# A Strassen-like fp32 MLP kernel without its 36 opening matmuls on ones

## The reference

```
h = jax.nn.gelu(jnp.einsum('bni,ih->bnh', x, W1) + b1, approximate=False)   # 512 -> 2048
shared_x = jnp.einsum('bnh,ho->bno', h, W2) + b2                             # 2048 -> 384
We_sel = We[indices]                                                         # one of 8 experts per batch
expert_x = jnp.einsum('bnh,bhp->bnp', h, We_sel) + be_sel[:, None, :]        # 2048 -> 128
out = x + jnp.concatenate([shared_x, expert_x], axis=-1)
```

## Time and profile before

| | |
|---|---|
| median of 3 runs | 1239.53 us (1239.34 to 1239.58) |
| the profiled execution, its own time | 1239.52 us |
| span of its profile | 1237.8 us |
| TensorE busy | 1232.1 us (100% of the span) |
| VectorE busy | 940.0 us (76%) |
| ScalarE busy | 742.4 us (60%) |
| TensorE's instructions | 9368 matmuls and 9368 weight loads |

### The profile page before, as it was taken

How to read it: one execution, slowest core, us unless ns; L and a number is a source line. 1 busy time by engine, 2 the same in 40 slices (tenths; PEclk the granted TensorE clock), 3 DMA queues, 4 the chain that set the end, 5 groups by cost and what they waited for, 6 DMA issues and landing times.

```text
span 1237.8 us, 23794 instructions
## 1 busy us (share of the span) xinstructions
PE 1232.1 (100%) x9368; PEld 917.4 (74%) x9368; DVE 940.0 (76%) x1201; ACT 742.4 (60%) x944; POOL 0.2 (0%) x4
## 2 busy tenths in 40 slices
PE   9999999999999999999999999999999999999998
PEld 4456667787787777777777877778778777777775
DVE  7986677877777877768878688787787777777765
ACT  4656556666566665666566566565666656666553
POOL 0000000000000000000000000000000000000000
PEclk9999999999999999999999999999999999999999
DMA  8223123012020110202002020030300203011000
GB/s 306 69 73 123 43 77 95 1 35 69 0 102 0 54 47 0 102 0 68 34 0 102 0 96 6 0 101 0 102 0 21 81 0 102 0 51 51 1 35 35
DMA packets 25234, 64.45 MB, mean 52 GB/s; under 512 B 5104, under 2 KB 5104, under 8 KB 22000
## 3 DMA queue, kind: packets, MB, share of 16 engines
q1 hardware_dynamic: 25200, 63.99, 15.1%
HBM read 47.20 MB, written 16.78 MB: 52 GB/s over the span
## 4 chain that ended last, share of the span: by engine, by line
PE 99%; DMA 1%; DVE 0%; SPq 0%; issue 0%
PE banks L1118 15%; PE banks L1119 15%; PE banks L1120 15%; PE out_ps L1120 9%; PE out_ps L1119 9%; PE out_ps L1118 9%; PE q_ps L1118 8%; PE q_ps L1119 8%; PE q_ps L1120 8%; PE banks L1132 1%; DMA h_ring<-w1f_dram 1%; PE out_ps L1132 0%; PE q_ps L1132 0%; SPq L356 0%; DVE x_raw L918 0%
## 5 line engine op out<-in xcount | busy, mean ns | idle before, releaser
L1120 PE MATMUL banks<-x_hi,w_lo 128*128 128x256 f16 (+1 forms) x1704 | 467.0, 274 | 0.0
L1119 PE MATMUL banks<-x_lo,w_hi 128*128 128x256 f16 (+1 forms) x1704 | 467.0, 274 | 0.0
L1118 PE MATMUL banks<-x_hi,w_hi 128*128 128x256 f16 (+1 forms) x1704 | 467.0, 274 | 0.0
L685 DVE SCALAR_TENSOR_TENSOR h_ring<-u,scale,h_ring 128x2048 f16<-128x2048 f32 x120 | 281.1, 2343 | 6.9 <-ACT h_ring L450 4.8
L517 ACT ACTIVATE kept<-banks 128x512 f32<-128x512 f32 x180 | 106.3, 591 | 170.3 <-PE banks L1120 170.3
L1118 PEld LDWEIGHTS banks<-x_hi,w_hi 128*128 128x128 f16 x1704 | 166.7, 98 | 44.1 <-ACT kept L517 0.5
L1119 PEld LDWEIGHTS banks<-x_lo,w_hi 128*128 128x128 f16 x1704 | 166.7, 98 | 43.2 <-issue 0.3
L1120 PEld LDWEIGHTS banks<-x_hi,w_lo 128*128 128x128 f16 x1704 | 166.7, 98 | 21.8
L458 ACT ACTIVATE h_ring<-u,scale 128x2048 f16<-128x2048 f32 x56 | 112.1, 2002 | 96.7 <-DVE u L861 96.7
L548 ACT ACTIVATE u<-u,b_sb,undo 128x512 f32<-128x512 f32 x120 | 91.2, 807 | 124.1 <-DVE u L906 124.1
L893 DVE TENSOR_TENSOR u<-banks,kept 128x512 f32<-128x512 f32 x60 | 41.5, 691 | 160.5 <-PE banks L1120 148.9
(11 more groups left out here) (142 smaller groups left out, 1664.9 us busy)
## 6 DMA issues: line engine op xcount, KB each, us to landing
e_raw<-we_dram SPq DMA_DIRECT2D x16, 1024.0 KB, 4.7
out_dram<-x_raw SPq DMA_DIRECT2D x64, 256.0 KB, 2.3
x_raw<-x_dram SPq DMA_DIRECT2D x60, 256.0 KB, 3.6
h_ring<-w_dram SPq DMA_DIRECT2D x5, 1024.0 KB, 7.7
t_sum<-w2p_dram SPq DMA_DIRECT2D x2, 1024.0 KB, 4.8
w_sums<-w_dram SPq DMA_DIRECT2D x2, 768.0 KB, 14.4
x_raw<-x_dram SPq DMA_DIRECT2D x2, 512.0 KB, 4.4
h_ring<-w1f_dram SPq DMA_DIRECT2D x2, 512.0 KB, 6.6
```

The costliest lines, as they stand in the source:

```text
L685: return nc.vector.scalar_tensor_tensor(to, of, s, hi, ALU.mult, ALU.subtract)
L1118: nc.tensor.matmul(ps, hi, v_hi, start=start, stop=False, skip_group_check=True)
L1119: nc.tensor.matmul(ps, hi, v_lo, start=False, stop=False, skip_group_check=True)
L1120: return nc.tensor.matmul(ps, lo, v_hi, start=False, stop=stop, skip_group_check=True)
```

## The change

The constant WARM and the loop on it are removed. TensorE still waits for `ones_set`, since the totals multiply by ones, and its first matmul is the total of x's maxima. Nothing else differs, except that the lines behind the removed ones carry smaller numbers (L1324 becomes L1321, and a line within the functions is one lower).

```
-WARM = 36
...
             pe.wait_ge(ones_set, 1)
-            for _ in range(WARM):
-                nc.tensor.matmul(out_ps[:, 1, :N // 2], ones[:, :P], ones[:, :], start=True, stop=True)
             pe.wait_ge(first_x_max_done, KC)
             total(first_x_tops, first_x_max[:, :]).then_inc(first_x_all_done, 1)
             first_batch()
```

## The result

| | before | after |
|---|---|---|
| median of 22 runs | 1239.55 us (1239.30 to 1239.99) | 1241.78 us (1240.74 to 1242.58) |
| ratio, 95% interval | | 1.0017 (1.0011 to 1.0023) |
| the profiled execution, its own time | 1239.52 us | 1241.97 us |
| its span | 1237.8 us | 1240.2 us |
| TensorE busy | 1232.1 us | 1229.1 us |

The change costs 2.2 us (0.18% by the medians, with an interval of 0.11% to 0.23%). That is inside the range of 1240.2 to 1242.8, but 0.8 us above the forecast of 1241.0: the loss is one and a half times the 1.44 us that were summed. TensorE is 3 us less busy and the kernel is slower. The runs of the changed kernel also lie over 1.84 us, those of before over 0.69.

The account below looks back on a forecast made before the run. TensorE was taken to bound the kernel from 7.97 us on. The terms 1.60 + 0.08 - 0.24 = +1.44 us on the profiled execution's 1239.52 gave 1241.0 us (+0.12%), range 1240.2 to 1242.8.

Parts of the forecast that it names:

- TensorE bounds the kernel from 7.97 us on: From the first float32 matmul TensorE works almost without pause; time lost there moves the end by as much.
- The ones' own work: Start, 1.19 to 6.86 us: removing 36 matmuls, 5.67 us of TensorE, gains 0, as VectorE's reduction and the DMA hide them.
- The rate behind it: First float32 matmuls, 7.97 to 11.2 us: TensorE at its lower level for 3.2 us, half of that lost, +1.60 us.
- The opening cost of +0.08: First float32 matmul: its extra distance of 0.07 to 0.08 us may double at the lower level, +0.08 us.
- The stall of -0.24: Total of W1's maxima, near 15 us: a later TensorE finds VectorE's maxima done and no longer waits, -0.24 us.
- The late stall near 205 us: Weight load waiting for ScalarE's copy `kept`, matmul 0.17 us late: moves with TensorE; between 0 and -0.17, taken as 0.
- VectorE and ScalarE: VectorE waits for the W1 total near 16.6 us and goes on some 0.6 later; no new wait comes up on TensorE.
- (a): Float32 start: slow stretch over 5.3 us, kernel slower by over 0.2%; at 6.4 us +3.04, 1242.6 us; chance 0.20.
- (b): Program start: slow first matmuls belong to it, TensorE at full rate at 7.97 us; no loss, 1239.5 us; chance 0.07.
- (c): Start: ones disturbed transfers or VectorE's reductions, W1 lands earlier without them; 0.01 for 2.5 us faster, faster in all 0.02.

Follow-up runs that it names:

- 36 + 64: Kernel before, its 36 opening matmuls kept, plus 64 matmuls on ones between the total of x's maxima and the first float32 matmul: 1246.04 us.
- with 28: Kernel before with 28 opening matmuls on ones in place of 36: 1239.50 us against 1239.59.
- with 54: Kernel before with 54 opening matmuls on ones in place of 36: 1240.27 us against 1239.59.
- the moved total: Kernel before with the total of W1's maxima one float32 product later: 1239.41 us against 1239.59, ratio 0.9999.
- 36 short ones: Kernel before, its 36 opening matmuls each cut from 256 columns of ones to 4: 1241.45 us against 1239.63.
- with 18: Kernel before with 18 opening matmuls on ones in place of 36: 1241.15 us against 1239.63.
- the 64: Changed kernel with 64 matmuls of 128x256 on ones between the total of x's maxima and the first float32 matmul: 1248.76 us.

## Why the prediction was right, and where it was off

- **TensorE bounds the kernel from 7.97 us on, and what it loses there moves the end.** Right: 2.46 us at 24.59 us, 2.45 at the end.
- **The ones' own work is worth 0.** Right: the total and the float32 matmuls start at 7.46 and 7.88 without them, against 7.29 and 7.97. The first is set by VectorE and the second by the DMA, which landed at 7.84 and 7.75; the landing alone moves by some tenths between executions, and this is part of every spread.
- **The rate behind it.** The mechanism was right: half the rate, until a rise, and with the level taken from distances against a clock column that says 1.00. The size was the step that was off: the term of +1.60 us, with 3.2 us of slow stretch taken from the one rise in the trace before. In the profiled execution of the changed kernel the stretch is 13.49 - 7.88 = 5.6 us, worth 2.8. Five traces that begin with the same ones at 1.19 us show how much it differs: 3.2 us before, and 4.8, 4.2, 3.4 and 5.6 us in the kernels with 36 + 64, with 28, with 54 and with the moved total. With the four that begin near 8 us (5.6 in the changed kernel, 6.2 with 36 short ones, 5.2 with 18 and 5.5 with the 64) the mean of nine is 4.9, and with it in place of 3.2 the sum gives 1241.8. Worked back from the times of its 22 runs, (time - 1239.55 + 0.24 - 0.06) x 2, the stretch of the changed kernel is 4.8 us in the middle, 2.7 for the fastest run and 6.4 for the slowest. This is an estimate: it puts all of a run's difference on the stretch, and the kernel before also varies by 0.69 us, worth 1.4 us of it.
- **The opening cost of +0.08.** Right in kind: the first two float32 records are 0.986 us apart and the others 0.853, so 0.13 in place of the 0.08 of before; the extra is 0.06.
- **The stall of -0.24.** Right, the total at 17.61 waits for nothing. The late stall near 205 us stayed, as taken, and moved with TensorE from 205.19 to 207.64 us. In the changed kernel nothing of the 0.24 is given back at x's second total, as it is with the moved total: the total stands at 27.18 us, 1.1 us behind VectorE's maximum (25.81 + 0.28).
- **VectorE and ScalarE.** Right in direction: VectorE waits 1.59 us at 17.82, more than the 0.6 expected as TensorE is later, and none of the deadlines behind it was missed (the first w_lo is done at 21.9 and TensorE reads it at 24.59).
- **The sum for the profiled execution**: 2.80 + 0.06 - 0.24 - 0.09 (the earlier start) = 2.53 against the measured 2.45.
- **The rivals.** (a), a stretch of over 5.3 us, was named as a sign that the forecast is wrong, and the profiled execution shows it with 5.6 us; by the estimate from the times 7 of the 22 runs do, and the median run doesn't. So it is not a rival but the upper part of the same distribution, and should have been written as a spread of the forecast and not as a case apart. The range was wide enough to hold the median because it had been drawn for other stretches than the one seen; the middle of 1241.0 rested on one draw, the shortest of the nine. The Trainium skill's remark in "TensorE: Matmul & The Clock Gate" (Part 1, "What's actually happening"), that the number of slow matmuls varies between runs of one kernel, is borne out by this case with profiled stretches of 3.2 to 6.2 us. Its transition at around 4 us gave an estimate of 1241.4, nearer than mine, but the plus or minus 0.5 us that it gives with it is far less than those stretches differ. (b) fell with the 36 short matmuls. (c) has nothing for it: the landing at 7.75 us without the ones is within the scatter.

Open: whether the slow stretch is longer when the work begins near 8 us than when it begins at 1.19. The five profiled stretches from 1.19 us on are 3.2 to 5.6 us, and the four that lie behind are 5.2 to 6.2. Worked back from the times, it is 3.6 us in the middle of the ten runs with 54 ones, and 4.8 in the middle of the 22 of the changed kernel. Both point the same way, but neither settles it, and what sets the length of a stretch stays open altogether. How long a pause may be is known at three places only. The 2.1 us behind 18 ones kept all 11 runs from being free of loss, whether or not the level had risen. The waits behind 28 (1.0 us before the total and 0.5 behind it) and behind 36 (0.4 and 0.5 us) did no harm in the profiled executions, after the level had risen.

## What to carry to other kernels

Work of no use that lies wholly in a wait of the bounding engine is free, and removing it can cost: ask what state the engine is in when the real work comes. Size such filler so that it is still running, or only just over, when the data lands, since too little (18 matmuls) helped hardly at all here and too much (54) cost its overhang, 0.7 us. Where a term depends on something that happens once in a profile, a single trace is one draw; give the term a range from the start, and its middle above the shortest seen.

## What the runs showed of the hardware

The time in which dense matmuls run at half rate before TensorE's level rises was 3.2, 3.4, 4.2, 4.8 and 5.6 us in five executions that all begin with the same matmuls on ones, and 5.2 to 6.2 us in four in which it was measured from about 8 us on. I had expected it to be nearly constant. Where an execution runs at half rate, its time is longer by half of that stretch: 2.8 us for 5.6 in the changed kernel. The profile's clock column reads 1.00 for all of it, because its first record begins with the rise (4.42 us before, 13.49 after the change). Distances between matmuls show the level (0.21 against 0.109 us for 256 columns in bfloat16, 0.853 against 0.43 for a float32 record), and so do weight loads of 128x128 in bfloat16 (151 against 98 ns). And the filler must be dense and in time: 36 instructions of 4 columns, and 18 of 256 followed by 2.1 us of nothing, left the float32 matmuls slow.
